# Flamingo cross-attention block on one core: how the reciprocals of the softmax row sums reach the context

## The reference, cut to what matters

```python
Q, K, V = proj(layernorm(x), q_w, q_b), proj(ctx, k_w, k_b), proj(ctx, v_w, v_b)
scores = where(mask, -1e9, Q @ K.T / sqrt(32))      # per batch and head: 512 x 512
attn = softmax(scores, axis=-1)                     # exp(s - max) / row sum
x = x + tanh(g_xattn) * (concat(attn @ V) @ o_w.T + o_b)
xn = layernorm(x); prev = xn shifted by one row
r = sigmoid(mix(xn, prev, mu_r) @ W_r.T); k = square(relu(mix(xn, prev, mu_k) @ W_k.T))
out = x + tanh(g_ffn) * r * (k @ W_v.T)
```

## Time and profile before

| | |
|---|---|
| median of three runs | 1231.34 us |
| profiled execution, its own time | 1232.68 us |
| its span, first to last instruction | 1230.8 us |
| PE busy | 1167.7 us, 95% |
| DVE busy | 942.5 us, 77% |
| ACT busy | 745.2 us, 61% |
| GpSimd busy | 237.4 us, 19% |
| DMA, the main queue's packets | 31.1% of 16 engines |
| TensorE clock granted, mean | 0.990 |

### The profile page before, as it was taken

One profiled execution on the slowest core, in us unless ns is written; L12 is line 12 of the kernel. 1 busy time (PEld: TensorE's weight loads), 2 busy tenths in 40 slices (PEclk: granted clock), 3 DMA queues, 4 the chain that ended last, 5 costly groups with the idle time before them and its releaser, 6 DMA issues.

```text
span 1230.8 us, 22178 instructions
## 1 busy us (share of the span) xinstructions
PE 1167.7 (95%) x7424; PEld 921.5 (75%) x7424; DVE 942.5 (77%) x2011; ACT 745.2 (61%) x1619; POOL 237.4 (19%) x427
## 2 busy tenths in 40 slices
PE   3999999999999999999999999977999999999997
PEld 2777776777777777777677777754888888888886
DVE  5778788788878887878878887879677677777763
ACT  4578778678768877877867876764432333233232
POOL 2030030030021003003003000024423433332431
PEclk9999999999999999999999999987999999999999
DMA  6433342253243333344225322452111311311200
GB/s 218 120 94 83 101 122 66 63 157 81 71 129 89 81 102 100 82 104 118 67 60 159 78 74 65 123 168 76 59 52 60 95 52 52 104 52 52 97 25 35
DMA packets 72703, 110.33 MB, mean 90 GB/s; under 512 B 14864, under 2 KB 23696, under 8 KB 72592
## 3 DMA queue, kind: packets, MB, share of 16 engines
q1 hardware_dynamic: 72592, 108.92, 31.1%
HBM read 41.76 MB, written 16.78 MB: 48 GB/s over the span
## 4 chain that ended last, share of the span: by engine, by line
PE 76%; DVE 9%; issue 6%; ACT 4%; DMA 4%; SPq 1%; POOL 0%; POOLq 0%; ACTq 0%; DVEq 0%
PE bank L445 24%; PE bank L509 14%; PE bank L476 12%; PE bank L521 10%; PE bank L502 7%; PE bank L485 6%; DMA x_rows<-x 3%; DVE neg_s L857 3%; ACT probs L681 2%; PE bank L491 2%; PE bank L575 1%; DVE pT L863 1%; DVE xh L973 1%; DMA pT<-wkT 1%; DVE ctx_sb L848 1%
## 5 line engine op out<-in xcount | busy, mean ns | idle before, releaser
L681 ACT ACTIVATE probs<-neg_s,negmax 128x512 f32<-128x512 f32 x512 | 367.9, 720 | 40.5 <-DVE negmax L857 39.4
L857 DVE CUSTOM_DVE_ANT_0 neg_s<-bank,mask_big 128x512 f32<-128x512 f32 x512 | 344.7, 683 | 19.2 <-PE bank L502 16.9
L509 PE MATMUL bank<-ident,probs 128*128 128x128 f32 x2048 | 314.8, 276 | 17.3 <-ACT probs L681 16.8
L509 PEld LDWEIGHTS bank<-ident,probs 128*128 128x128 f32 x2048 | 240.4, 141 | 75.6 <-ACT probs L681 40.7
L863 DVE COPY pT<-bank 128x512 f32<-128x512 f32 x256 | 176.5, 690 | 120.8 <-PE bank L509 119.7
L502 PE MATMUL bank<-k_stack,q_stack 96*128 96x512 f32 x512 | 243.3, 475 | 6.0 <-DVE negmax L857 5.9
L688 ACT COPY pT<-bank 128x512 f32<-128x512 f32 x256 | 149.4, 584 | 98.3 <-PE bank L509 92.5
L1068 POOL TENSOR_SCALAR var_eps<-mv 128x2 f32<-128x2 f32 (+1 forms) x24 | 18.5, 770 | 639.9 <-DVE mv L822 578.3
L521 PE MATMUL bank<-pT,v_sb 128*32 128x512 f32 x1024 | 118.5, 603 | 0.8 <-issue 0.5
L779 ACT ACTIVATE relu<-bank 128x512 f32<-128x512 f32 x32 | 19.2, 598 | 149.0 <-PE bank L445 149.0
L502 PEld LDWEIGHTS bank<-k_stack,q_stack 96*128 96x128 f32 x512 | 97.3, 190 | 11.2 <-DVE negmax L857 8.5
(11 more groups left out here) (110 smaller groups left out, 2125.1 us busy)
## 6 DMA issues: line engine op xcount, KB each, us to landing
k_stack<-k_hi SPq DMA_DIRECT2D x256, 64.0 KB, 2.0
q_stack<-q_hi SPq DMA_DIRECT2D x256, 64.0 KB, 2.0
x_rows<-x SPq DMA_DIRECT2D x8, 1024.0 KB, 6.6
cT_raw<-ctxT SPq DMA_DIRECT2D x8, 1024.0 KB, 5.8
k_stack<-k_lo SPq DMA_DIRECT2D x128, 64.0 KB, 2.0
q_stack<-q_lo SPq DMA_DIRECT2D x128, 64.0 KB, 2.0
ctx_dram<-ctx_sb SPq DMA_DIRECT2D x32, 256.0 KB, 2.1
c_raw<-ctx_dram SPq DMA_DIRECT2D x16, 512.0 KB, 5.1
```

What stands on the lines that cost most here:

```text
L509: mm = nc.tensor.transpose(pt_bank[i % 2][:, a * P:(a + 1) * P], probs[:, i % P_RING, a * P:(a + 1) * P], ident[:])
L681: nc.scalar.activation(probs[:, i % P_RING, :], neg_s[:, i % SM_RING, :], ACT.Exp, bias=negmax[:, k:k + 1], scale=-1.0, accum_out=den[:, g ...
L857: nc.vector.tensor_tensor_reduce(neg_s[:, i % SM_RING, :], s_bank[i % S_BANKS][:], mask_big[:, q, :], 1.0, 3e38, ALU.add, ALU.min, negmax[ ...
```

## The change

`rden_rep`, its copy (L873), three of the four transposes of item R, ACT's copy (L672) and DVE's product at step 2 go. In their place:

- PE transposes `rden` itself, 128 x 16, into 16 rows of 128 of the side bank: one transpose.
- DVE copies these 16 rows to SBUF at step 2 of the next group.
- SP stores them in DRAM (`store_rden`, 8 KB) at the place where it stored the context. Behind the first nine or twelve q copies it waits for that store to land, and loads them back with four DMAs (`load_rden`), each of which spreads one head's 512 reciprocals over 32 partitions of `rden_bc`.
- DVE multiplies `pv_bank` by `rden_bc` behind step 7 (`divide`). It waits for the four loads.
- SP stores the context behind all stack copies of the group, where it waits for that product.
- PE's next context waits for the product and no longer for item R. ACT waits once for the last context ahead of stage 2.

The loops over the batches are written without their split-off last pass, which leaves the order on each engine as it was.

```diff
-        rden_rep = sb(stage1, "rden_rep", [P, TT, GH, HD])
+        rden_bc = sb(stage1, "rden_bc", [P, S])
+        rden_rows = [ctx_sb[0:TILES, s, 0:P] for s in range(2)]
...
                 stack_q(b, n, range(first))
+                if b * GROUPS + n > 1:
+                    load_rden(b * GROUPS + n - 2)
                 stack_k(b, n, (0,))
...
+            def store_rden(b, c):
+                sp.wait_ge(side_done, done(side_no(b, ("R", c))))
+                sp.dma_start(rden_dram[b * GROUPS + c].rearrange("(r q) -> r q", r=TILES),
+                             rden_rows[c % 2]).then_inc(rden_st, 16)
+            def load_rden(g):
+                sp.wait_ge(rden_st, (g + 1) * 16)
+                sp.wait_ge(ctx_done, g)
+                for j in range(GH):
+                    sp.dma_start(rden_bc[j * HD:(j + 1) * HD, :],
+                                 rden_dram[g:g + 1, j * S:(j + 1) * S].to_broadcast([HD, S])).then_inc(rden_ld, 16)
             def store_context(b, c):
-                sp.wait_ge(side_done, done(side_no(b, ("R", c))))
+                sp.wait_ge(ctx_done, b * GROUPS + c + 1)
...
-                    if c:
-                        store_context(b, c - 1)
+                    if b + c:
+                        store_rden(*((b, c - 1) if c else (b - 1, GROUPS - 1)))
...
                         stack_group(b, c + 1)
+                    else:
+                        load_rden(b * GROUPS + c - 1)
+                    if b + c:
+                        store_context(*((b, c - 1) if c else (b - 1, GROUPS - 1)))
...
-                    for q in range(TT):
-                        mm = nc.tensor.transpose(bank[:, q * P:(q + 1) * P],
-                                                 rden_rep[:, q].rearrange("p j d -> p (j d)"), ident[:])
+                    mm = nc.tensor.transpose(bank[0:TILES, 0:P], rden[:], ident[:])
...
-                if kind == "R":
-                    nc.scalar.copy(ctx_sb[:, n % 2, :], bank[:]).then_inc(side_hi, 1)
...
+                if kind == "R":
+                    dve.wait_ge(side_mm, mm_no(b, item) + 1)
+                    dve.wait_ge(ctx_st[n % 2], (b * 2 + n // 2) * 16 + DMA_HEAD)
+                    nc.vector.tensor_copy(rden_rows[n % 2], bank[0:TILES, 0:P]).then_inc(side_done, 1)
...
+            def divide(b, c):
+                g = b * GROUPS + c
+                dve.wait_ge(rden_ld, (g + 1) * GH * 16)
+                dve.wait_ge(pv_mm, g + 1)
+                nc.vector.tensor_tensor(ctx_sb[:, c % 2, :], pv_bank[:], rden_bc[:], ALU.mult).then_inc(ctx_done, 1)
...
-                nc.vector.reciprocal(rden[:], den[:, c % 2, :]).then_inc(rden_calc, 1)
-                dve.wait_ge(rden_calc, g + 1)
-                src = rden[:].rearrange("p (j q) -> p q j", j=GH)[:, :, :, None].to_broadcast([P, TT, GH, HD])
-                nc.vector.tensor_copy(rden_rep[:], src).then_inc(rden_ready, 1)
+                nc.vector.reciprocal(rden[:], den[:, c % 2, :]).then_inc(rden_ready, 1)
...
                         tile_step(b, c, i)
+                        if b and (c, i) == (0, LO_STEP):
+                            side(b - 1, "R", GROUPS - 1)
+                        if b + c and i == DIVIDE_STEP:
+                            divide(*((b, c - 1) if c else (b - 1, GROUPS - 1)))
```

More of the change, by code:

```diff
@@ L260, in hi_no @@
             if b is None:
-                return [i for i in PROLOGUE if i[0] != "V"].index(item)
-            order = [i for i in (ORDER_LAST if isinstance(b, int) and b == B - 1 else ORDER) if i[0] != "V"]
+                return [i for i in PROLOGUE if i[0] not in "VR"].index(item)
+            order = [i for i in (ORDER_LAST if b == B - 1 else ORDER) if i[0] not in "VR"]
             return b * HI_PER_BATCH + HI_PROLOGUE + order.index(item)
@@ L410, in batch @@
                         load_w2(3)
-                store_context(b, GROUPS - 1)
-            for b in range(B - 1):
+            for b in range(B):
                 batch(b)
-            batch(B - 1)
+            store_rden(B - 1, GROUPS - 1)
+            load_rden(B * GROUPS - 1)
+            store_context(B - 1, GROUPS - 1)
             for s in range(2):
@@ L428, in step2 @@
                              o_sb[:, h]).then_inc(out_st[h], 16)
-            for b in range(B - 1):
+            for b in range(B):
                 step2(b, 0)
                 step2(b, 1)
-            step2(B - 1, 0)
-            step2(B - 1, 1)
             for s in range(2):
@@ L712, in tile_step @@
                     probs_out(b, c, i)
[L714 to L719, removed]
             def batch(b):
                 for c in range(GROUPS):
-                    for i in range(EARLY if c == 0 else 0, TILES):
+                    for i in range(TILES):
                         tile_step(b, c, i)
@@ L749, in context_hi @@
                 nc.scalar.copy(c_hi[:], c_raw[:, h]).then_inc(c2_hi, 1)
-            early_steps(0)
-            for b in range(B - 1):
+            for b in range(B):
                 batch(b)
-            batch(B - 1)
             def xT_out(b, h):
@@ L1042, in _ @@
             mixed_lo(0, 0, 0)
-            for b in range(B - 1):
+            divide(B - 1, GROUPS - 1)
+            for b in range(B):
                 step2(b, 0)
                 step2(b, 1)
-            step2(B - 1, 0)
-            step2(B - 1, 1)
         @block.gpsimd
@@ L1161 @@
     ctx_dram = nc.dram_tensor("ctx_dram", (B * D, S), F32, kind="Internal").ap()
-    build(nc, *args, out, ctx_dram)
+    rden_dram = nc.dram_tensor("rden_dram", (B * GROUPS, TILES * P), F32, kind="Internal").ap()
+    build(nc, *args, out, ctx_dram, rden_dram)
     result = run_bass_kernel_spmd(nc, [arrays], core_ids=[0])
```

61 lines of the change are left out of this document (22 added, 39 removed).

## The result

The changed kernel takes 1359.49 us, the median of four runs from 1355.41 to 1364.90. The kernel before took 1231.63 us beside it. The ratio is 1.1041 (95% interval 1.1001 to 1.1081): 128 us slower. The forecast was 1353.

A forecast was written before the change was run, and what follows sets the result against it. The prediction took PE's stream, with small holes, to bound stage 1, DVE running only two tiles ahead. 1232.7 - 14 (gain) + 94 (stalls) + 42 (clock) = 1354.7, runs' median 1.3 lower: 1353 us; own range 1335 to 1375, whole range 1292 to 1388.

The forecast's parts named there:

- The gain: Item R and removed copies: three transposes fewer in 32 groups, 9.3 us, plus 4.7 us in c = 2 groups; 14 us.
- The copy at step 2: DVE's added 16 x 128 copy: 0.30 us, ending 0.38 us earlier than the product it replaces.
- my X: Time the last load has landed: slot - 0.38 + 3 x 0.63 + landing; 355.4, 378.3, 404.3, 427.0 in groups 12 to 15.
- What waits: DVE's product behind tile 9's mask stands still for 4.6, 2.3 and 4.4 us in groups 12 to 14; ACT and PE wait.
- X + 2.2: Start of PE's tile 10, 2.2 us after the last load lands; 2.9 us late in group 13, 3.2 in group 14.
- The stalls' sum: PE's delays from late loads over all groups and the end of stage 1: 94 us, bounds 64 to 115.
- The clock: PE's clock falls to half after nine stalls over 4 us and ten of about 3: 42 us, bounds 0 and 90.
- SP's longer series: SP issues 30 instead of 25 DMAs in a group, 18.6 us at 0.62; the rest of its series stays hidden.
- rival 1: Stalls, but no fall of the clock in most groups: 1313 us, down to 1285 with shorter load slots; chance 0.22.
- rival 2: Longer clock falls: 24 stalls at 4 us are 96, time 1409; with half of them, 1385; chance 0.13.
- rival 4: Half the stall: load slot 0.35 and landing 1.9, 22 stalls shrink by 0.9; 1293 us, 1315 with some falls; chance 0.12.
- Rival 3: Faster SP issue lets the loads land before DVE's product; only the gain is left, 1219 us; chance 0.04.

The follow-up runs named there:

- The transposes alone: Kernel before, with item R doing only the first of its four transposes and all else the same: 1223.80 us, ratio 0.9926.
- the kernel with PE kept busy: Changed kernel plus 20, 10 and 10 useless PE matmuls ahead of tile 12's scores (c = 0, 1, 2; batches 0 to 6): 1332.61 us, ratio 1.0817.

## Why the prediction was right

**The gain.** Forecast 14 us, measured 16 to 19. The transposes alone are 9.9 (9.3 forecast). The part beside them was put at 4.7, all of it in the groups with c = 2, and is 6 to 9: 3.3 us where c = 2, 3.4 where c = 0, which I had left out, and 2 to 3 in group 31. The late k copies take some of it back. In the changed kernel the stalls swallow the part where c = 0 or 2: it lies ahead of tile 10, and tile 10 starts 2.2 us after the loads have landed, however early PE gets there. The sum took it off all the same.

**The copy at step 2.** Taken as 0.30 us, measured 0.272.

**When the loads land.** A load's slot was put at 0.63 us and is 0.47, the first of four 0.57: four take 1.92 us where I had 2.5. The landing of 2.1 lies in the bounds. Against that the q copies ahead are slower than before, nine in 5.98 us or 0.66 each in group 13. The product starts 14.7, 12.4 and 13.7 us after the first transposes of groups 12, 13 and 14; my X, taken the same way, was 14.9, 12.1 and 14.8. The two errors offset each other in the first two.

**What waits.** DVE's waits were put at 4.6, 2.3 and 4.4 us and are 5.48, 3.15 and 3.74. The first two were misread. The product stands behind tile 9's mask, but the rows that I took in groups 12 and 13 (ends at 350.76 and 375.96) are tile 10's masks. Tile 9's in group 12 is the one before:

```profile
349.46 0.68 DVE L857 CUSTOM_DVE_ANT_0 neg_s<-bank,mask_big 128x512 f32<-128x512 f32 x1
```

It ends at 350.14, and that of group 13 at 375.34. With these and the same X, the waits come out at 5.3 and 3.0 us. The sum does not suffer from it, since it took PE's delay from X + 2.2 and not from DVE's wait. That step held: with PE at the full clock it is 2.2 us in each of the 20 stalled groups of batches 0 to 6. Outside the last batch the landing varies by up to 1.2 us between groups of one kind. In the seven groups with c = 3 ahead of the last batch, DVE waits 0.4 to 1.5 us, 0.95 in the mean, and PE loses 0.5 in the mean. So there is slack, but it is 0.5 us where c = 3, 1.2 where c = 2 and none where c = 0 or 1, and not about a tile.

**The stalls' sum.** Forecast 94 us. The changed kernel is 144 us slower than the same kernel with the product behind step 13 (1359.5 against 1214.5 to 1216.4), and 27 of these are the clock's in batches 0 to 6. That leaves 117, in which the last batch's falls are still hidden. Their price is an estimate: PE is busy 27.8 us at half clock in the changed kernel's last batch and 12.3 in that of the kernel with step 13, and half of the difference is 8 us at most. So the stalls are 109 to 117 us, and this term was too small by a seventh to a fifth. By kind, from the tiles' starts in the kernel with PE kept busy against the one with step 13, up to tile 15: c = 0 5.9 us in each of six groups (5.2 forecast; group 0 has no product), c = 1 3.6 (2.9), c = 2 4.3 (3.2), c = 3 0.5 (0.1), the last batch 23 in all (17, with groups 28 to 31). Where c = 0 or 2, 0.4 to 0.5 us of that is the swallowed gain. Where c = 1 the loads land 0.5 us later in the mean than I had. Where c = 2, 1.2 us stand behind tile 10, where DVE also has `k_lo` to make up for; that it is the cause was not tested. In group 31 the small store took 5 us to land behind the weight load, and SP issues the loads only at 951.04 after the store at 946.07. I had 2.1:

```profile
946.07 0.50 SPq L381 DMA_DIRECT2D rden_dram<-ctx_sb  x1
951.04 1.72 SPq L389 DMA_DIRECT2D rden_bc<-rden_dram  x4
```

**The clock.** Forecast 42 us, measured 27 in batches 0 to 6 and at most 35 with the last: too large by a fifth to a half. All 23 stalled groups with c = 0, 1 and 2 and group 31 have a fall where I let 19 have one. That is the rule of the Trainium skill, "TensorE: Matmul & The Clock Gate", section "HAM oscillation", and this trace agrees with it: 24 of 24. But one fall cost less than my 2.0 to 2.5 us. Batches 0 to 6 have 20 stretches at 0.50 in the changed kernel and one with PE kept busy, so it is 27 / 19 = 1.4 us. PE is busy for 93.7 of the 112.6 us of these 20 stretches. I counted half of such busy time as lost, which would be 47 us. Where c = 1 that is nearly so (14.8 us measured from the product's start to tile 15, half of the busy time is 16.7). Where c = 2 it is 6.9 of 16.8, and where c = 0 it is 4.9 of 13.3. That PE would wait there for DVE at the full clock too was not traced.

**Luck.** The gain was put 2 to 5 us too small, the stalls 15 to 23 too small and the falls 7 to 15 too large. These cancelled in part, and the total is nearer the mark than its two large terms. The mechanism and the path were right.

**SP's longer series.** Put at nothing. For the changed kernel that holds: PE waits for no stack copy in its trace. In the kernel with step 13, where PE runs without stalls, the k copies behind the loads come late and cost 3.4 us.

**The rivals.** The clock does fall, so rival 1 is out; no fall in batches 0 to 6 cost the 4 us that rival 2 asks (2.8 at most, from the product's start to tile 15); the load slot of 0.47 is a step towards rival 4, but was offset by the q copies. Rival 3, the loads in time, is what two of the experiments made of the kernel; the change as it stands is not that.

## What to carry to other kernels

A DMA round trip inside a tight pipeline is cheap if nothing waits for it before it lands and the DMAs behind it in the queue can spare its issue slots; the distance to count is from the issue slot behind everything already queued on the issuing engine, not from the point where the data is ready. Before a wait is put on an in-order engine, compare that landing with the point at which the engine gets there: here six steps later turned 10% slower into 1.3 to 1.5% faster. What a wait costs is the wait less the slack ahead of the engine that has none to spare, and the slack differs by place: here between 0 and 1.2 us. A hole on PE is paid for again when the clock falls, for half of PE's busy time at half clock at most. Before you change the order of work for a wait, look at what landed just before it ended.

## What the runs showed of the hardware

- DMA issues on one queue do not all cost the same, and the same DMA costs more right behind another. Right behind another: 0.59 us for an SBUF to SBUF copy of 64 KB, 0.42 for a load of 64 KB from DRAM with a repeated row, 0.50 for the 8 KB store, 0.58 for the 256 KB store. After a pause of the queue: 0.31 for the 8 KB store, 0.33 for the 256 KB store (kernel before). About 0.04 us come between two in a row.
- A row of 2 KB in DRAM spread over 32 partitions lands in 2.1 us, like a plain copy of the same size (2.0); four such rows in one DMA of 256 KB need 5.6 us from issue to use.
- The small store (8 KB) lands in 1.4 us where no large transfer is ahead of it, in 5.0 behind a 1 MB weight load (group 31) and in 6.2 behind the 1 MB x load (group 12).
- In the changed kernel the granted clock fell from 2.4 to 1.2 GHz in all 24 groups in which PE stood still for 2.3 to 8.1 us before the scores of tile 12, and in none of the three with 0.6 to 0.7 us. The length of the hole alone does not decide it: with the loads ahead of the q copies, a hole of 2.2 us was followed by no fall (group 8), and one of 1.2 us by 3.4 us at 0.50 (group 12).
